# Second attention of a four-layer graph network: rows gathered per group of edges, block numbers loaded behind the next one-hot

## The chip, the cores and the metric

One NeuronCore of a Trainium2 chip runs the whole network as one program. The metric is the time of one execution on the device in microseconds (us), the median of some runs. Five engines work side by side, each with an instruction stream of its own and waiting for the others on semaphores: TensorE (PE, matrix products and transposes), VectorE (DVE), ScalarE (ACT), GpSimd (POOL, which here issues the gathers of rows) and SyncE (SP, plain DMAs).

## The reference

3125 nodes with 128 features, 50000 edges sorted by their target node. Four layers follow one another; the first two are attentions over edges:

```python
# first attention, H = 2 heads of 128
xl, xr = (h @ Wl + bl), (h @ Wr + br)
e = leaky_relu(xl[src] + xr[dst], 0.2)
alpha = segment_softmax(einsum('ehd,hd->eh', e, att), dst)
out = segment_sum(xl[src] * alpha[..., None], dst).mean(axis=1)
# second attention, one head
m = leaky_relu(xl[src] + xr[dst] + edge_weight @ We, 0.2)
alpha = segment_softmax(m @ att, dst)
out = segment_sum(xl[src] * alpha[:, None], dst)
```

Three GINE layers (message `relu(x[src] + e)`, sum by target, two dense layers, a batch norm) and an edge network with a node network end it. Each layer is followed by a residual sum and a layer norm.

## The kernel before

The edges are cut into 98 groups of 512. The nodes are cut into 25 blocks of 128. An item is a group together with one block of targets: a group whose targets cross from one block to the next is worked on twice, and so there are 98 + 24 = 122 items. `groups_blocks` holds for item i the group, its place in a ring of eight (`group & 7`), the block, and the block of item i - 2 (for the accumulation that lags two items). `group_end` holds for each group the number of items up to its last.

An attention (`gat_edges`, number 0 with two heads, number 1 with one) runs all 122 items in a pipeline that `walk` writes out: five items in full, then a loop with four items a turn, then the last. On each engine a step does `front` of item i, `tail` of item i - 2, `back` of item i - 1 and `mid` of item i. For one item and head:

- GpSimd gathers the source rows of 4 x 128 edges with four indirect DMAs (L760) into one of four buffers, after the products (L807) of the item four before have read it. An item that shares its group with the one before gathers the same rows again.
- TensorE transposes the rows (L772), ScalarE copies the transposes to `vs` (L820). TensorE adds the target side as three products with a one-hot matrix `hot_t` and, in the second attention, the edge weight (L780, L782).
- VectorE adds the two (L881, "the sum"), applies the leak (L885), makes the one-hot matrix of the next item (L863). TensorE multiplies by the attention vector (L790, "the scores").
- VectorE masks the scores and takes their maximum (L894, "the masked maximum"), and brings the running maximum up to date in three small steps (L901, L904, L906), whose addresses depend on the item's block number. ScalarE takes exponentials (L837, L840), TensorE transposes them (L799), ScalarE copies (L844), TensorE multiplies them with the gathered rows (L807), VectorE accumulates rows and sums into the place of the block (L917, L918). ScalarE makes the mask of the next item (L825).

VectorE needs the block numbers of items i and i - 2 as registers for these addresses. `read_blocks` (L865 to L873) loads both at once from `groups_blocks`; its instructions carry L871. It stands in `front` between the sum and the leak of the first head. L182 and L188 are lines of the helpers `wait` and `hold`, which issue waits and bring their values into registers.

In the GINE layers (L988) the rows are already gathered once per group into `ring`, the same memory seen as eight places of 4 x 128 rows of 128 features.

Of the kernel before, what the change touches and what calls it, by code (L numbers as in the profile page):

```python
# [23 lines left out]
ACT = mybir.ActivationFunctionType  # L24
AX = mybir.AxisListType.X

P = 128
NODES, EDGES, D = 3125, 50000, 128
EDGE_D, HID, HEADS, GINE_LAYERS = 32, 256, 2, 3
NODE_BLOCKS = -(-NODES // P)  # L30
# [3 lines left out]
SUBS = 4  # L34
# [48 lines left out]
def build(nc, t):  # L83

    with ExitStack() as ctx:
# [3 lines left out]
        def sem(name):  # L89
            return ctx.enter_context(nc.semaphore(name))  # L90
# [616 lines left out]
        rel_in = [sem(f"rel_in{s}") for s in range(2)]  # L707
        gathered = [sem(f"gathered{s}") for s in range(4)]


# [4 lines left out]
        def gat_edges(number, heads, dram, att, with_weight, target, sp_head=None, dve_head=None):  # L715
# [4 lines left out]
            name = f"gat{number}"  # L720
            w_in = [sem(f"{name}_w_in{s}") for s in range(2)] if with_weight else []
            cleared, hot_t_done, negs, g_ready, g_copied, v_ready, v_added, leaked, s_ready, s_masked, neg_max_new, max_step, max_done, p_ready, scl_ready, \
                pt_ready, pt_copied, o_ready, acc_done = gat_sems
# [10 lines left out]
            with nc.Block() as block:  # L734
# [20 lines left out]
                @block.gpsimd  # L755
                def _(pool):
                    for i in range(ITEMS):
                        wait(pool, o_ready, before_h + heads * (i - 3))
                        for j in range(SUBS):
                            pool.indirect_dma_start(  # L760
                                out=gath[:, i % 4, j, 0:width], out_offset=None, in_=dram,
                                in_offset=bass.IndirectOffsetOnAxis(ap=idx_all[:, i, j:j + 1], axis=0)).then_inc(gathered[i % 4], 16)

                @block.tensor
                def _(e):
                    def front(i, s, turn, s4, turn4):

                        e.wait_ge(gathered[s4], 16 * SUBS * (turn4 + 1))
                        for h in range(heads):
                            wait(e, pt_copied, before_h + heads * (i - 2) + h + 1)  # L770
                            for j in range(SUBS):
                                last = e.transpose(T[h][:, j * P:(j + 1) * P], gath[:, s4, j, h * D:(h + 1) * D], ident)  # L772
                            last.then_inc(g_ready, 1)
# [28 lines left out]
                    def tail(i, s, turn, s4, turn4):  # L802
                        wait(e, acc_done, before + i)
                        for h in range(heads):
                            e.wait_ge(pt_copied, before_h + heads * i + h + 1)
                            for j in range(SUBS):
                                last = e.matmul(O[h], pt[:, h, j, :], gath[:, s4, j, h * D:(h + 1) * D],  # L807
                                                start=(j == 0), stop=(j == SUBS - 1))
                            last.then_inc(o_ready, 1)
# [5 lines left out]
                def _(a):  # L815
                    def front(i, s, turn, s4, turn4):
                        for h in range(heads):
                            wait(a, leaked, before_h + heads * (i - 1) + h + 1)
                            a.wait_ge(g_ready, before_h + heads * i + h + 1)
                            a.activation(vs[:, h, :], T[h], ACT.Copy).then_inc(g_copied, 1)  # L820

                    def mask(i, s, turn):
# [4 lines left out]
                    def mid(i, s, turn, s4, turn4):  # L827

                        if not (isinstance(i, int) and i == ITEMS - 1):
                            mask(i + 1, 1 - s, turn + s)  # L830

                    def back(i, s, turn, s4, turn4):
# [13 lines left out]
                    target.scalar(a)  # L846
                    mask(0, 0, number * PAIRS)
                    walk(a, front, back, mid, layer=number)

                @block.vector  # L850
                def _(v):
# [23 lines left out]
                    def front(i, s, turn, s4, turn4):  # L875

                        for h in range(heads):
# [3 lines left out]
                            v.tensor_tensor(vs[:, h, :], V[h], vs[:, h, :], ALU.add).then_inc(v_added, 1)  # L881
                            if h == 0:
                                read_blocks(i)
                            v.wait_ge(v_added, before_h + heads * i + h + 1)
                            v.scalar_tensor_tensor(lk[:, h, :], vs[:, h, :], 0.2, vs[:, h, :], ALU.mult, ALU.max).then_inc(leaked, 1)  # L885
                        if not (isinstance(i, int) and i == ITEMS - 1):
                            make_hot_t(i + 1, 1 - s, turn + s)

                    def mid(i, s, turn, s4, turn4):
# [38 lines left out]
        gi_ea = [sem(f"gine_ea_in{s}") for s in range(2)]  # L928
        gi_gath = [sem(f"gine_gathered{s}") for s in range(RING)]
        gi_landed, gi_free = sem("gine_landed"), sem("gine_free")  # L930
# [7 lines left out]
        def gine_edges(layer):  # L938
# [8 lines left out]
            with nc.Block() as block:  # L947
                def landings(slot, round):

                    return 16 * SUBS * (layer * -(-(GROUPS - slot) // RING) + round + 1)  # L950

# [119 lines left out]
        def mlp_edges(target):  # L1071
# [4 lines left out]
            ea_before, rel_before = 16 * GINE_LAYERS * PAIRS, 16 * 2 * PAIRS  # L1076
            gathered_before = [16 * SUBS * 2 * -(-(ITEMS - m) // 4) for m in range(4)]
            cleared, hot_t_done, hot_done, counted, h1_ready, h1_added, turned, h1_done, h2_ready, h2_added, h2_done, o_ready, acc_step = (
# [819 lines left out]
```

## Time and profile before

| | us |
|---|---|
| median of 3 runs (lowest, highest) | 4297.36 (4291.48, 4302.65) |
| the profiled execution, its own time | 4295.06 |
| its span, first to last instruction | 4293.3 |
| busy in the span: PE, DVE, POOL, ACT | 3411.3, 2638.0, 2554.6, 1615.8 |
| first attention, sums from 106.2 on, last leak at | 911.5 |
| second attention, first leak, last leak at | 990.5, 1602.4 |

The span covers all layers one after another, so a share of busy time over the span is a mean over stages with different limits. The windows of a stage, the waits in it and the timeline of single items are read for what holds within the stage. An engine's name with a q at its end (DVEq, POOLq) is its sequencer: waits, register steps and loads, which aren't counted as busy.

### The profile page before, as it was taken

To read this page: it belongs to the slowest core of one execution; us is meant where nothing else is said; L and a number is where in the kernel's file an instruction comes from. 1 tells how busy PE (TensorE), PEld (TensorE's weight loads), DVE (VectorE), ACT (ScalarE), POOL (GpSimd) and SP (SyncE) were. 2 spreads that over 40 slices of the span, in tenths; PEclk is the share of its full clock that TensorE was granted. 3 is DMA by queue.
4 is the path that set the end of the run, shared out by engine and by line. 5 is a ranking of instruction groups with operands and counts; after the bars stand their busy time and mean duration, and the time that the engine had idled before them with its cause. 6 is when DMAs were issued, how large, how long until landed. Compare 5 with 4: busy or idle time off the path is not lost. (4 is left out here: it accounts for less than half of the span.)

```text
span 4293.3 us, 91716 instructions
## 1 busy us (share of the span) xinstructions
PE 3411.3 (79%) x20792; PEld 2646.5 (62%) x20793; DVE 2638.0 (61%) x6163; ACT 1615.8 (38%) x3137; POOL 2554.6 (60%) x2650
## 2 busy tenths in 40 slices
PE   6999999977788774676656566666666999999996
PEld 3777777754555543555545445455544888888894
DVE  5888888875666664343334333343345888888884
ACT  3666666644555553111121111211114333333334
POOL 4555555536777766777757777577772444444430
PEclk7999999988999995555566655555567999999998
DMA  3333333322322221222222222222222333333330
GB/s 118 89 98 100 100 99 99 101 69 63 80 80 81 80 70 57 68 68 68 67 62 68 67 67 68 60 69 69 67 68 73 112 107 107 111 107 107 111 90 15
DMA packets 293250, 349.78 MB, mean 81 GB/s; under 512 B 63536, under 2 KB 236755, under 8 KB 292915
## 3 DMA queue, kind: packets, MB, share of 16 engines
q0 software_dynamic: 98528, 229.12, 18.7%
q1 hardware_dynamic: 140481, 92.05, 7.8%
q10 hardware_dynamic: 54162, 27.77, 2.3%
q8 instruction: 24, 0.39, 0.0%
q14 instruction: 55, 0.45, 0.0%
HBM read 332.61 MB, written 16.07 MB: 81 GB/s over the span
## 5 line engine op out<-in xcount | busy, mean ns | idle before, releaser
L988 POOL DMA_INDIRECT gath<-source_rows_narrow,gine_idx x1176 | 1141.9, 971 | 426.7 <-issue 357.4
L1036 DVE TENSOR_TENSOR vs<-psum,gath 128x512 f32<-128x512 f32 x366 | 252.9, 691 | 802.3 <-SPq L973 673.7
L1142 POOL DMA_INDIRECT gath<-source_rows,idx_all x416 | 429.5, 1032 | 507.6 <-DVE vs L1263 351.9
L1002 PE MATMUL psum<-gine_lin,ea 32*128 32x128 f32 x2928 | 278.7, 468 | 543.2 <-DVE vs L1036 513.6
L760 POOL DMA_INDIRECT gath<-source_rows,idx_all x488 | 463.7, 950 | 378.1 <-PE psum L807 263.2
L760 POOL DMA_INDIRECT gath<-source_rows_narrow,idx_all x488 | 463.4, 950 | 207.1 <-issue 134.8
L1002 PEld LDWEIGHTS psum<-gine_lin,ea 32*128 32x128 f32 x2928 | 177.4, 286 | 642.0 <-DVE vs L1036 574.7
L790 PE MATMUL psum<-lk,att_b 128*128 128x512 f32 x732 | 376.4, 621 | 113.9 <-DVE lk L885 113.2
L807 PEld LDWEIGHTS psum<-gath,pt 128*128 128x128 f32 x2928 | 365.1, 192 | 36.8 <-DVE zsum L918 1.8
L1066 ACT ACTIVATE pm<-vs 128x512 f32<-128x512 f32 x186 | 117.1, 630 | 693.3 <-DVE vs L1036 686.6
L1167 PE MATMUL psum<-weight_all,pm 128*128 128x256 f32 x1664 | 377.2, 380 | 0.0
L1011 PE MATMUL psum<-hot,pm 128*128 128x128 f32 x1488 | 355.9, 414 | 19.9 <-ACT pm L1066 19.0
L807 PE MATMUL psum<-gath,pt 128*128 128x128 f32 x2928 | 366.4, 275 | 0.8 <-ACT pt L844 0.8
L1011 PE MATMUL psum<-lk,sm 128*128 128x128 f32 x1440 | 350.4, 420 | 4.4 <-ACT sm L1066 3.1
L885 DVE SCALAR_TENSOR_TENSOR lk<-vs 128x512 f32<-128x512 f32 x366 | 253.4, 692 | 160.1 <-DVE vs L881 150.9
L1011 PEld LDWEIGHTS psum<-hot,pm 128*128 128x128 f32 x1488 | 305.1, 304 | 63.1 <-DVE ACC L1045 46.8
L1066 ACT ACTIVATE sm<-vs 128x512 f32<-128x512 f32 x180 | 113.4, 630 | 607.9 <-DVE vs L1036 546.0
L1167 PEld LDWEIGHTS psum<-weight_all,pm 128*128 128x128 f32 x1664 | 308.7, 191 | 39.0
L1011 PEld LDWEIGHTS psum<-lk,sm 128*128 128x128 f32 x1440 | 301.4, 310 | 45.1 <-ACT sm L1066 20.8
L820 ACT ACTIVATE vs<-psum 128x512 f32<-128x512 f32 x366 | 205.4, 595 | 290.5 <-PE psum L772 290.5
L844 ACT ACTIVATE pt<-psum 128x512 f32<-128x512 f32 x366 | 205.5, 595 | 270.2 <-PE psum L799 261.0
L894 DVE CUSTOM_DVE_ANT_0 sm<-psum,neg 128x512 f32<-128x512 f32 x366 | 244.8, 686 | 94.2 <-PE psum L790 91.6
(241 smaller groups left out, 6143.6 us busy)
## 6 DMA issues: line engine op xcount, KB each, us to landing
rel<-rel_rows SPq DMA_DIRECT2D x244, 128.0 KB
ea<-in_edge_attr_tiles SPq DMA_DIRECT2D x416, 64.0 KB
ea<-in_edge_attr ACTq DMA_DIRECT2D x366, 64.0 KB
gath<-source_rows_narrow,gine_idx POOLq DMA_INDIRECT x1176
gath<-source_rows,idx_all POOLq DMA_INDIRECT x904
rel<-quad_rel_rows SPq DMA_DIRECT2D x104, 128.0 KB
gath<-source_rows_narrow,idx_all POOLq DMA_INDIRECT x488
source_rows<-ACC SPq DMA_DIRECT2D x12, 512.0 KB, 2.9
```

The costliest lines, as they stand in the source:

```text
L760: pool.indirect_dma_start(out=gath[:, i % 4, j, 0:width], out_offset=None, in_=dram, in_offset=bass.IndirectOffsetOnAxis(ap=idx_all[:, i, ...
L790: e.matmul(S[h], att_b[:, att[h], :], lk[:, h, :], start=True, stop=True).then_inc(s_ready, 1)
L807: last = e.matmul(O[h], pt[:, h, j, :], gath[:, s4, j, h * D:(h + 1) * D], start=(j == 0), stop=(j == SUBS - 1))
L885: v.scalar_tensor_tensor(lk[:, h, :], vs[:, h, :], 0.2, vs[:, h, :], ALU.mult, ALU.max).then_inc(leaked, 1)
L894: v.tensor_tensor_reduce(out=sm[:, h, :], in0=S[h], in1=neg[:, s, :], scale=1.0, scalar=-4 * MASK, op0=ALU.subtract, op1=ALU.max, accum_ou ...
L988: pool.indirect_dma_start(out=ring[:, g % RING, j, :], out_offset=None, in_=table1, in_offset=bass.IndirectOffsetOnAxis(ap=gine_idx[:, g, ...
L1002: last = e.matmul(E[:, j, :], ea[rows, s, :], gine_lin[rows, layer, :], start=True, stop=True)
L1011: last = e.matmul(O[s4], pms[s4][:, j * P:(j + 1) * P], hots[s4][:, j, :], start=(j == 0), stop=(j == SUBS - 1))
L1036: v.tensor_tensor(vs[:, s, :].rearrange("p (j d) -> p j d", j=SUBS), E, ring[:, bass.ds(slot, 1), :, :].rearrange("p a j d -> p (a j) d"), ...
L1066: a.activation(pms[s4], vs[:, s, :], ACT.Relu).then_inc(gi["msg"], 1)
L1142: pool.indirect_dma_start(out=gath[:, q % 4, j, :], out_offset=None, in_=table, in_offset=bass.IndirectOffsetOnAxis(ap=quad_idx[:, q, j:j ...
L1167: last = e.matmul(H2[:, j, :], h1[:, h, j * P:(j + 1) * P], w2[h], start=(h == 0), stop=(h == 1))
```

## The change

In the second attention GpSimd gathers each group once, into the ring of eight, in 4 indirect DMAs for each of 98 groups. Ahead of a group's gathers (from the ninth group on) it loads the group's last item and waits until that item's rows are taken; behind them it waits for the group before to land and says so (`rows_landed`). ScalarE copies an item's rows from the ring to one of four buffers (`rows`, in the unused half of `ACC`), one item ahead, behind the copy of the transposes. It loads the item's group and ring place ahead of that copy. TensorE reads the rows from there. In both attentions `read_blocks` moves from between the first head's sum and leak to behind the next item's one-hot. The waits of later layers are renumbered.

```diff
--- before.py
+++ after.py
@@ -706,6 +706,8 @@
 
         rel_in = [sem(f"rel_in{s}") for s in range(2)]
         gathered = [sem(f"gathered{s}") for s in range(4)]
+        gi_gath = [sem(f"group_gathered{s}") for s in range(RING)]
+        rows_landed, rows_taken, slot_free = (sem(f"gat1_{k}") for k in ("rows_landed", "rows_taken", "slot_free"))
 
 
         gat_sems = [sem(f"gat_{k}") for k in (
@@ -719,6 +721,8 @@
             acc = ACC[:, 0:NODE_BLOCKS * width].rearrange("p (b h d) -> p b h d", h=heads, d=D)
             name = f"gat{number}"
             w_in = [sem(f"{name}_w_in{s}") for s in range(2)] if with_weight else []
+            by_group = heads == 1
+            rows = ACC[:, NODE_BLOCKS * D:NODE_BLOCKS * D + 4 * GROUP_EDGES].rearrange("p (s j d) -> p s j d", s=4, j=SUBS) if by_group else gath
             cleared, hot_t_done, negs, g_ready, g_copied, v_ready, v_added, leaked, s_ready, s_masked, neg_max_new, max_step, max_done, p_ready, scl_ready, \
                 pt_ready, pt_copied, o_ready, acc_done = gat_sems
             before = number * ITEMS
@@ -754,6 +758,25 @@
 
                 @block.gpsimd
                 def _(pool):
+                    def report(g):
+                        pool.wait_ge(gi_gath[g % RING], 16 * SUBS * (g // RING + 1))
+                        pool.nop().then_inc(rows_landed, 1)
+
+                    if by_group:
+                        pool.wait_ge(gine_idx_in, 16)
+                        for g in range(GROUPS):
+                            if g >= RING:
+                                end = pool.value_load(group_end[0:1, g - RING:g - RING + 1], min_val=1, max_val=ITEMS)
+                                pool.wait_ge(rows_taken, end)
+                                pool.nop().then_inc(slot_free, 1)
+                            for j in range(SUBS):
+                                pool.indirect_dma_start(
+                                    out=ring[:, g % RING, j, :], out_offset=None, in_=dram,
+                                    in_offset=bass.IndirectOffsetOnAxis(ap=gine_idx[:, g, j:j + 1], axis=0)).then_inc(gi_gath[g % RING], 16)
+                            if g >= 1:
+                                report(g - 1)
+                        report(GROUPS - 1)
+                        return
                     for i in range(ITEMS):
                         wait(pool, o_ready, before_h + heads * (i - 3))
                         for j in range(SUBS):
@@ -765,11 +788,14 @@
                 def _(e):
                     def front(i, s, turn, s4, turn4):
 
-                        e.wait_ge(gathered[s4], 16 * SUBS * (turn4 + 1))
+                        if by_group:
+                            e.wait_ge(rows_taken, i + 1)
+                        else:
+                            e.wait_ge(gathered[s4], 16 * SUBS * (turn4 + 1))
                         for h in range(heads):
                             wait(e, pt_copied, before_h + heads * (i - 2) + h + 1)
                             for j in range(SUBS):
-                                last = e.transpose(T[h][:, j * P:(j + 1) * P], gath[:, s4, j, h * D:(h + 1) * D], ident)
+                                last = e.transpose(T[h][:, j * P:(j + 1) * P], rows[:, s4, j, h * D:(h + 1) * D], ident)
                             last.then_inc(g_ready, 1)
 
                         b = block_of(e, i)
@@ -804,7 +830,7 @@
                         for h in range(heads):
                             e.wait_ge(pt_copied, before_h + heads * i + h + 1)
                             for j in range(SUBS):
-                                last = e.matmul(O[h], pt[:, h, j, :], gath[:, s4, j, h * D:(h + 1) * D],
+                                last = e.matmul(O[h], pt[:, h, j, :], rows[:, s4, j, h * D:(h + 1) * D],
                                                 start=(j == 0), stop=(j == SUBS - 1))
                             last.then_inc(o_ready, 1)
 
@@ -814,10 +840,15 @@
                 @block.scalar
                 def _(a):
                     def front(i, s, turn, s4, turn4):
+                        taken = by_group and not (isinstance(i, int) and i == ITEMS - 1)
+                        if taken:
+                            place_of_rows = load_place(i + 1)
                         for h in range(heads):
                             wait(a, leaked, before_h + heads * (i - 1) + h + 1)
                             a.wait_ge(g_ready, before_h + heads * i + h + 1)
                             a.activation(vs[:, h, :], T[h], ACT.Copy).then_inc(g_copied, 1)
+                        if taken:
+                            take(i + 1, (s4 + 1) % 4, *place_of_rows)
 
                     def mask(i, s, turn):
                         a.wait_ge(rel_in[s], 16 * (turn + 1))
@@ -828,6 +859,19 @@
 
                         if not (isinstance(i, int) and i == ITEMS - 1):
                             mask(i + 1, 1 - s, turn + s)
+
+                    def load_place(i):
+                        _, (g, slot) = nc.values_load_multi_w_load_instructions(
+                            groups_blocks[0:1, bass.ds(i, 1), 0:2], engines=(mybir.EngineType.Activation,),
+                            min_val=0, max_val=GROUPS - 1)
+                        return g, nc.s_assert_within(slot, 0, RING - 1)
+
+                    def take(i, s4, g, slot):
+                        a.wait_ge(rows_landed, g + 1)
+                        if not isinstance(i, int) or i >= 4:
+                            a.wait_ge(o_ready, before_h + i - 3)
+                        a.activation(rows[:, s4, :, :], ring[:, bass.ds(slot, 1), :, :].rearrange("p a j d -> p (a j) d"),
+                                     ACT.Copy).then_inc(rows_taken, 1)
 
                     def back(i, s, turn, s4, turn4):
 
@@ -845,6 +889,8 @@
 
                     target.scalar(a)
                     mask(0, 0, number * PAIRS)
+                    if by_group:
+                        take(0, 0, *load_place(0))
                     walk(a, front, back, mid, layer=number)
 
                 @block.vector
@@ -879,12 +925,11 @@
                             v.wait_ge(v_ready, before_h + heads * i + h + 1)
                             v.wait_ge(g_copied, before_h + heads * i + h + 1)
                             v.tensor_tensor(vs[:, h, :], V[h], vs[:, h, :], ALU.add).then_inc(v_added, 1)
-                            if h == 0:
-                                read_blocks(i)
                             v.wait_ge(v_added, before_h + heads * i + h + 1)
                             v.scalar_tensor_tensor(lk[:, h, :], vs[:, h, :], 0.2, vs[:, h, :], ALU.mult, ALU.max).then_inc(leaked, 1)
                         if not (isinstance(i, int) and i == ITEMS - 1):
                             make_hot_t(i + 1, 1 - s, turn + s)
+                        read_blocks(i)
 
                     def mid(i, s, turn, s4, turn4):
                         b = blocks["item"]
@@ -926,7 +971,6 @@
         gi = {k: sem(f"gine_{k}") for k in (
             "hot_done", "e_ready", "added", "msg", "o_ready", "acc_done", "cleared")}
         gi_ea = [sem(f"gine_ea_in{s}") for s in range(2)]
-        gi_gath = [sem(f"gine_gathered{s}") for s in range(RING)]
         gi_landed, gi_free = sem("gine_landed"), sem("gine_free")
 
         def group_of(e, i):
@@ -947,7 +991,7 @@
             with nc.Block() as block:
                 def landings(slot, round):
 
-                    return 16 * SUBS * (layer * -(-(GROUPS - slot) // RING) + round + 1)
+                    return 16 * SUBS * ((layer + 1) * -(-(GROUPS - slot) // RING) + round + 1)
 
                 def by_group(e, body):
 
@@ -1074,7 +1118,7 @@
             acc = ACC[:, :].rearrange("p (h b n) -> p b h n", h=2, n=P)
             ea_in = gi_ea
             ea_before, rel_before = 16 * GINE_LAYERS * PAIRS, 16 * 2 * PAIRS
-            gathered_before = [16 * SUBS * 2 * -(-(ITEMS - m) // 4) for m in range(4)]
+            gathered_before = [16 * SUBS * -(-(ITEMS - m) // 4) for m in range(4)]
             cleared, hot_t_done, hot_done, counted, h1_ready, h1_added, turned, h1_done, h2_ready, h2_added, h2_done, o_ready, acc_step = (
                 sem(f"mlp_{k}") for k in ("cleared", "hot_t_done", "hot_done", "counted", "h1_ready", "h1_added", "turned", "h1_done", "h2_ready", "h2_added",
                                           "h2_done", "o_ready", "acc_step"))
```

## Rows read from the trace of the kernel before

**Rows 1.** Windows view, both attentions: us; busy PE, PEld, DVE, ACT, POOL; clock, DMA share, GB/s.
```profile
97.00:902.00 805.00, 794.47 (x5012) 585.71 (x5013) 660.53 (x1917) 514.27 (x1198) 447.30 (x472) 0.99 0.35 97
970.00:1607.00 637.00, 504.82 (x2714) 317.24 (x2713) 399.96 (x1232) 336.15 (x742) 454.78 (x479) 0.98 0.29 76
```

**Rows 2.** Waits view, second attention: waiter, releaser, total us, times, longest.
```profile
DVE lk L885 <- DVE vs L881: 77.2, 119, 1.0
```

**Rows 3.** Timeline of VectorE, four items of the first attention: start, us.
```profile
502.38 0.69 DVE L881 TENSOR_TENSOR vs<-psum,vs 128x512 f32<-128x512 f32 x1
...
512.08 0.69 DVE L885 SCALAR_TENSOR_TENSOR lk<-vs 128x512 f32<-128x512 f32 x1
...
515.89 0.69 DVE L881 TENSOR_TENSOR vs<-psum,vs 128x512 f32<-128x512 f32 x1
517.21 0.69 DVE L885 SCALAR_TENSOR_TENSOR lk<-vs 128x512 f32<-128x512 f32 x1 [0.62 <-DVE vs L881]
517.81 0.68 DVE L881 TENSOR_TENSOR vs<-psum,vs 128x512 f32<-128x512 f32 x1
518.53 0.69 DVE L885 SCALAR_TENSOR_TENSOR lk<-vs 128x512 f32<-128x512 f32 x1
...
520.18 0.68 DVE L894 CUSTOM_DVE_ANT_0 sm<-psum,neg 128x512 f32<-128x512 f32 x1
...
522.32 0.69 DVE L881 TENSOR_TENSOR vs<-psum,vs 128x512 f32<-128x512 f32 x1
...
528.72 0.69 DVE L881 TENSOR_TENSOR vs<-psum,vs 128x512 f32<-128x512 f32 x1
```

**Rows 4.** Line L871, VectorE's sequencer, 515.8 to 517.2: ns min/median/max, first, last start.
```profile
L871 DVEq FUSED_REGOPS  x3: 81/197/209, 515.9 to 516.9; - x3
...
L871 DVEq TENSOR_LOAD <-groups_blocks x1: 530/530/530, 516.0 to 516.0; - x1
```

**Rows 5.** Lines L188 and L182 on VectorE's sequencer, five narrow windows.
```profile
L188 DVEq FUSED_REGOPS  x1: 154/154/154, 513.2 to 513.2; - x1
...
L188 DVEq FUSED_REGOPS  x1: 154/154/154, 519.4 to 519.4; - x1
...
L182 DVEq EVENT_SEMAPHORE  x1: 50/50/50, 519.7 to 519.7; - x1
...
L188 DVEq FUSED_REGOPS  x1: 154/154/154, 1286.1 to 1286.1; - x1
...
L188 DVEq FUSED_REGOPS  x1: 154/154/154, 1301.6 to 1301.6; - x1
```

**Rows 6.** Timeline, second attention: VectorE over four items, then all engines, 1286 to 1289.
```profile
1284.21 0.69 DVE L881 TENSOR_TENSOR vs<-psum,vs 128x512 f32<-128x512 f32 x1
...
1287.57 0.69 DVE L894 CUSTOM_DVE_ANT_0 sm<-psum,neg 128x512 f32<-128x512 f32 x1 [0.70 <-PE psum L790]
...
1289.07 0.69 DVE L881 TENSOR_TENSOR vs<-psum,vs 128x512 f32<-128x512 f32 x1
...
1300.69 0.69 DVE L885 SCALAR_TENSOR_TENSOR lk<-vs 128x512 f32<-128x512 f32 x1 [0.62 <-DVE vs L881]
...
1304.33 0.69 DVE L881 TENSOR_TENSOR vs<-psum,vs 128x512 f32<-128x512 f32 x1
...
1286.27 1.13 PE L790 MATMUL psum<-lk,att_b 128*128 128x512 f32 x2 [0.84 <-DVE lk L885]
...
1286.47 0.94 POOL L760 DMA_INDIRECT gath<-source_rows_narrow,idx_all  x1 [0.30 <-issue]
...
1287.87 0.60 ACT L820 ACTIVATE vs<-psum 128x512 f32<-128x512 f32 x1 [1.20 <-PE psum L772]
...
1288.61 0.72 ACT L837 ACTIVATE pm<-sm,small 128x512 f32<-128x512 f32 x1
```

**Rows 7.** Lines L947 and L988: end of the first edge layer on GpSimd.
```profile
L947 POOLq DRAIN  x1: 19265/19265/19265, 2141.0 to 2141.0; - x1
...
L988 POOL DMA_INDIRECT gath<-source_rows_narrow,gine_idx x392: 940/945/2119, 1656.9 to 2155.0; - x196
```

## Prediction

> **What bounds the kernel now.** I read the windows of the two attentions first, then the waits of VectorE in them, then the timeline of single items, then the sequencer's own instructions. In the first attention TensorE is busy for 794 of 805 us, in the second for 505 of 637, with the clock fully granted in both [rows 1]. So at first sight TensorE bounds the first attention and something else the second. The waits and the timelines show one pause that both share: the leak (L885) waits for the sum before it (L881) once an item, for some 77 us in total in the second, 0.62 us a time in both [rows 2, 3, 6]. That isn't the sum's latency, because the second head has the same pair without a pause (517.81 to 518.53 is the sum's own 0.68 us) [rows 3]. It is the load of two block numbers: its instructions begin at 515.9, right behind the sum, and go on into the second half of the pause [rows 3, 4].
>
> Of one item of the first attention the reader should see VectorE's order: sum, leak, sum, leak, next one-hot, two pairs of accumulations (L917, L918), then the two masked maxima (L894), then the three small steps, and the next sum. The item begun at 515.89 has its first masked maximum at 520.18 (4.29 later), and the next item begins at 522.32 (2.14 after that): 6.43. VectorE's only pause of size in it is the 0.62 [rows 3]. Four items (one turn of the loop) take 528.72 - 502.38 = 26.34, 6.585 each, so three items go at VectorE's 6.4 and the one with the loop's branch takes 7.06. TensorE's own work is at most 794.47 / 122 = 6.51 an item [rows 1]. The first attention is bound by both engines at once, and VectorE has nothing to give away.
>
> In the second attention four items take 1304.33 - 1284.21 = 20.12, or 5.03 each [rows 6]. The ring of one item is: sum, load, leak, scores on TensorE (L790, 1286.27), the next item's transposes (L772) and products (L782) behind them, the next sum at 1289.07. A gather costs GpSimd 0.94 and 0.30 of issue, 1.245, and four of them 4.98 [rows 6]: GpSimd is a second bound, 0.05 behind the first. Neither half of the change would bring much by itself there.
>
> **GpSimd, part by part.** 488 gathers become 392: 98 groups x 4.98 = 488 us, from 959 us on, 4.0 for each of the 122 items. Each group adds one load of a number, two waits and two signals. The load that the trace prices, VectorE's, takes 1.26 for two numbers (from 515.9 until the leak is issued at 517.2) [rows 3, 4]. From below it is free: the closing drain of the first edge layer starts on GpSimd's sequencer at 2141.0, while the last gather starts at 2155.0, so the sequencer runs eleven gathers ahead of the engine [rows 7], and the wait for the group before ends while the engine still has gathers of this group. From above the whole 1.26 is exposed: 98 x 6.24 = 612, 5.01 an item, and the gain of this attention is gone. I take free, for the sequencer's lead is shown. 5.0 to 4.0 takes GpSimd off the path.
>
> **ScalarE.** It gains one copy of 128x512 in each item of the second attention, and a load of two numbers. The nearest row for the copy is the transposed rows' copy, 0.60 [rows 6]. It goes behind that copy (L820) and ahead of the exponential (L837), which now starts 0.74 after L820. Counted from the item's first sum in the new ring: scores at 1.46, L820 1.60 after them (1286.27 to 1287.87) at 3.06, the new copy to 4.3, the exponential and its sum 0.82 (estimate from its 0.72) to 5.15, its four transposes, 0.65 with their start, to 5.9. The next scores stand behind them on TensorE and are due at 4.78 + 1.46 = 6.24. So 0.3 are left, and the copy is covered. The loads lie under the mask of 0.71 and in the idle 1.20 ahead of L820 [rows 6]. The copy's wait for the group has a ring of eight groups ahead of it. ScalarE's busy time goes from 336 by 122 x 0.6 = 73 to 409 of 637 [rows 1]: not a bound. Price 0; if the copy came onto the ring in full, +0.6 an item, which is the upper end. TensorE waits for this copy in place of the gather, one item ahead. Its first copy adds under 1 us at the start, hidden by VectorE's clearing of the accumulator.
>
> **VectorE, the decisive part.** The load leaves the place between sum and leak and goes behind the issue of the next one-hot. Between these places VectorE's sequencer waits for the last sum, so its lead is gone when the load begins; behind the load stand the waits and address steps of the accumulations and of the masked maximum. The sequencer does one after the other. Its time there: the last leak starts at 518.53, the address step L188 ahead of the masked maximum at 519.4, 0.87 later, and an item before 512.08 and 513.2, 1.12. I take the middle, 0.99. In the second attention it is 0.91 (1300.69 to 1301.6) and 0.58 (1286.1, with the leak 0.74 ahead of its scores at 1286.27), the middle 0.74 [rows 3, 5, 6]. L188 takes 0.154; the wait behind it starts at 519.7, 0.3 after L188; and the masked maximum starts about 0.13 later (estimate, from 1287.57 and its wait) [rows 5]. So 0.43 from L188 to the masked maximum.
>
> First attention, from the item's first sum: leak at 0.73, second sum at 0.73 + 0.60, last leak at 2.05 (from 517.21, 517.81, 518.53), then 0.99 + 1.26 + 0.43: masked maximum at 4.73 where it is at 4.29. The 0.6 is gained ahead of the last leak, but the engine then runs dry under the load (one-hot done at about 3.0, first accumulation at 3.8). +0.44 an item; in the loop's branch item some 0.12 of waiting for the second head's scores drops out, 0.03 an item. TensorE, ACT and GpSimd follow. 121 x 0.41 = **+50 us**.
>
> Second attention: leak at 0.73, masked maximum at 0.73 + 0.74 + 1.26 + 0.43 = 3.16 where it is 3.36 (1284.21 to 1287.57); the next sum 1.50 after it (1287.57 to 1289.07), and 0.12 for the branch (0.47 in one of four): 4.78 in place of 5.03. TensorE's ring would allow less: 0.73 + 0.72 + 2.80 = 4.25, 4.39 with the branch. 108 items x 0.25 = 27; the first twelve pay a further 5 for gathers that come late, which the ring of eight takes away. **-32 us.**
>
> Sum +18 on the profiled execution's 4295.06 (span 4293.3 and 1.8 around it), which is 2.3 under the median of three: 4315 us on the median's basis.
>
> A load of two numbers takes 0.530 on VectorE's sequencer, without the address steps around it [rows 4]. The Trainium skill ("DMA: Bandwidth & Descriptors", section "Latency and other measured facts") puts the floor of a tensor_load at about 600 ns; the row is under it. By the page the load behind the one-hot would be 0.07 longer in each of 229 items, 16 us more than by the row; the row is of the same instruction, and decides.
>
> **Rivals.** About 0.3% (13 us) is what a measurement of this kernel can tell from no change.
> A, forecast: the load is serial on the sequencer in both attentions, +50 - 32. With +-0.07 an item on some 240 items 4298 to 4332. Chance 0.50, 0.15 of it within 0.3%, whose upper end is 4310.
> B: it is serial, but my sequencer distances are 0.1 to 0.2 too long, for address steps may be cheaper behind a load. Each 0.1 is worth 24 us over both attentions, +18 - 36 in the middle: 4279, 4267 to 4300. For it: the distances differ by 0.25 to 0.33 between items of one loop. Chance 0.24, 0.16 of it within 0.3%.
> C, the other side: the load lies wholly under the leak and one-hot (0.60 + 0.35 of engine time against 1.26) and the idle 0.70 ahead of the masked maximum. Then the first attention goes at TensorE's pace, 26.34 to some 26.18 per four items, -5 us, and the second at TensorE's 4.39: 108 x 0.64 + 10 = -79. 4213. It decides where the load leaves the masked maximum where it was. For it: the second attention has that idle time. Against: the first has none, and there its 0.31 beyond the engine time and 0.9 of steps behind it can't hide. Chance 0.18, with parts of it up to 4262.
> D: GpSimd's load or ScalarE's copy is exposed, the second attention gains nothing: 4297 + 50 = 4347, past the upper end of the range. Chance 0.08.
>
> **Numbers.** Predicted 4315. The range, 4260 to 4338, leaves out C's core and D. Slower by over 0.3%: A 0.35 and D 0.08, 0.43. Within: A 0.15 and B 0.16, 0.31. Faster: B 0.08 and C 0.18, 0.26.
>
> **What would show it.** The leak's pause gone in both (0.62 to nothing); in its place a pause of VectorE between the one-hot and the first accumulation, some 0.8 in the first attention. Four items of the first attention in 28.0, of the second in 19.1. TensorE's busy share of the first falls from 0.99. GpSimd waits for the ring in the second. If the first attention keeps 26.3, the step on the sequencer is wrong; if the second keeps 20, look at the exponential and the new copy.

## The result, and the profile after

The changed kernel takes 4306.28 us (median of 15 runs, 4300.59 to 4309.84), the kernel before, beside it on the same chip, 4296.24 (15 runs, 4291.41 to 4302.65): a ratio of 1.0021, 95% interval 1.0014 to 1.0028. That is 10 us slower: clear of the scatter of the runs, but within the 0.3% that the prediction counts as no change. Predicted were +18 us and "slower by over 0.3%" as the likeliest. The time lies in the stated range; the change is not the one that was held likeliest.

The windows of the changed kernel, cut at the same places of the work as those of [rows 1] (columns as there):
```profile
97.00:943.00 846.00, 819.67 (x4961) 579.74 (x5021) 677.09 (x1919) 528.18 (x1201) 467.91 (x472) 0.99 0.34 92
1010.00:1617.00 607.00, 515.79 (x2683) 320.24 (x2714) 414.09 (x1231) 396.05 (x865) 372.53 (x384) 0.98 0.28 70
```
Beside [rows 1], the first window has grown by 41 us and the second has shrunk by 30. From the first sum to the last, it is 802.7 to 842.9 us (+40.3) in the first attention and 611.5 to 581.9 (-29.6) in the second. In the second GpSimd's busy time falls from 455 to 373 us, for 98 groups in place of 122 items, and ScalarE's rises from 336 to 396, for the copies out of the ring. Two effects of opposite sign stand behind a total that looks like nothing. In the first window TensorE's busy time grows from 794 to 820 us for the same products, so busy time isn't a fixed amount of work. The 794 of 805 in [rows 1] doesn't by itself show TensorE's own pace; the run with the load taken apart, below, does.

VectorE's timeline, one item of the first attention (lines have moved: the sum is L927, the leak L929, the one-hot L909, the accumulations L962 and L963, the masked maximum L939, the load of the block numbers L917):
```profile
522.94 0.69 DVE L927 TENSOR_TENSOR vs<-psum,vs 128x512 f32<-128x512 f32 x1
523.66 0.69 DVE L929 SCALAR_TENSOR_TENSOR lk<-vs 128x512 f32<-128x512 f32 x1
524.27 0.68 DVE L927 TENSOR_TENSOR vs<-psum,vs 128x512 f32<-128x512 f32 x1
524.99 0.69 DVE L929 SCALAR_TENSOR_TENSOR lk<-vs 128x512 f32<-128x512 f32 x1
525.60 0.35 DVE L909 TENSOR_SCALAR hot_t<-rel,consts 128x512 bf16<-128x512 bf16 x1
526.81 0.35 DVE L962 SCALAR_TENSOR_TENSOR ACC<-ACC,factors,psum 128x128 f32 x1 [0.86 <-issue]
...
527.66 0.69 DVE L939 CUSTOM_DVE_ANT_0 sm<-psum,neg 128x512 f32<-128x512 f32 x1
...
530.31 0.69 DVE L927 TENSOR_TENSOR vs<-psum,vs 128x512 f32<-128x512 f32 x1 [0.55 <-issue]
...
550.84 0.69 DVE L927 TENSOR_TENSOR vs<-psum,vs 128x512 f32<-128x512 f32 x1
```
The 0.62 between sum and leak of [rows 3] is gone: the first leak starts 0.72 after its sum. Behind the one-hot stands a new pause of 0.86, from 525.95 to 526.81, released by "issue": VectorE's own sequencer isn't ready. The load and its steps take the sequencer from 525.24 to 526.47:
```profile
L917 DVEq FUSED_REGOPS  x3: 75/197/209, 525.2 to 526.2; - x3
...
L917 DVEq TENSOR_LOAD <-groups_blocks x1: 527/527/527, 525.4 to 525.4; - x1
```
The load itself (0.53 from 525.35) still runs under the last leak and the one-hot. What falls into the pause are its address steps (525.91 to 526.47) and, behind them on the same sequencer, the waits and the address step of the first accumulation.

Four items, 522.94 to 550.84, take 27.90, from 26.34 before. In the second attention one item reads:
```profile
1319.57 0.69 DVE L927 TENSOR_TENSOR vs<-psum,vs 128x512 f32<-128x512 f32 x1
1320.30 0.69 DVE L929 SCALAR_TENSOR_TENSOR lk<-vs 128x512 f32<-128x512 f32 x1
1320.91 0.35 DVE L909 TENSOR_SCALAR hot_t<-rel,consts 128x512 bf16<-128x512 bf16 x1
1322.12 0.35 DVE L962 SCALAR_TENSOR_TENSOR ACC<-ACC,factors,psum 128x128 f32 x1 [0.87 <-issue]
...
1322.71 0.69 DVE L939 CUSTOM_DVE_ANT_0 sm<-psum,neg 128x512 f32<-128x512 f32 x1
...
1324.67 0.69 DVE L927 TENSOR_TENSOR vs<-psum,vs 128x512 f32<-128x512 f32 x1 [0.50 <-PE psum L808]
...
1338.74 0.69 DVE L927 TENSOR_TENSOR vs<-psum,vs 128x512 f32<-128x512 f32 x1
```
The masked maximum comes 3.14 after the sum (3.36 in [rows 6]), and four items, 1319.57 to 1338.74, take 19.17, from 20.12. The waits of the second attention agree:
```profile
DVE ACC L962 <- issue: 103.6, 120, 1.2
...
POOL gath L773 <- ACT ACC L873: 74.2, 40, 4.1
```
The 77 us in front of the leak [rows 2] are gone and 104 us in front of the first accumulation have come. That the item is shorter all the same comes from the masked maximum: in the kernel before VectorE waits for its scores as well, 0.70 in [rows 6], 86.7 us in the whole window of the second attention; in the changed kernel these waits are down to 5.2.
```profile
DVE sm L894 <- PE psum L790: 86.7, 121, 2.0
```
The scores now start 0.6 earlier, with the leak, and are ready when the sequencer is. The leak's pause and this wait shrink by more than the new pause costs. GpSimd now waits for a free place in the ring (L873 is ScalarE's copy out of it): it is off the path.

### The profile page after: what moved, and what is told of

Its sections match the earlier page's. It is cut to its first block and busy times, and to the rows that moved or that the text cites. A ratio compares the mean times of both kernels' runs of the same rounds, so it can differ in the third digit from the quotient of the medians.

```text
span 4298.8 us, 93469 instructions
## 1 busy us (share of the span) xinstructions
PE 3466.9 (81%) x20700; PEld 2662.1 (62%) x20793; DVE 2668.6 (62%) x6163; ACT 1687.9 (39%) x3259; POOL 2491.2 (58%) x2554
## 5 line engine op out<-in xcount | busy, mean ns | idle before, releaser
L1032 POOL DMA_INDIRECT gath<-source_rows_narrow,gine_idx x1176 | 1140.7, 970 | 426.3 <-issue 357.5
L1186 POOL DMA_INDIRECT gath<-source_rows,idx_all x416 | 429.5, 1033 | 507.1 <-DVE vs L1307 352.0
L783 POOL DMA_INDIRECT gath<-source_rows,idx_all x488 | 484.3, 992 | 399.2 <-PE psum L833 284.6
L773 POOL DMA_INDIRECT gath<-source_rows_narrow,gine_idx x392 | 380.4, 971 | 217.3 <-issue 99.3
L816 PE MATMUL psum<-lk,att_b 128*128 128x512 f32 x732 | 400.0, 634 | 60.2 <-DVE lk L929 59.3
L1055 PE MATMUL psum<-hot,pm 128*128 128x128 f32 x1488 | 367.0, 424 | 18.0 <-ACT pm L1110 17.6
L1055 PEld LDWEIGHTS psum<-hot,pm 128*128 128x128 f32 x1488 | 314.9, 313 | 61.3 <-DVE ACC L1089 43.4
L881 ACT ACTIVATE pm<-sm,small 128x512 f32<-128x512 f32 x366 | 262.0, 716 | 122.5 <-DVE small L946 119.0
L927 DVE TENSOR_TENSOR vs<-psum,vs 128x512 f32<-128x512 f32 x366 | 252.3, 689 | 41.3 <-PE psum L808 18.8
L808 PE MATMUL psum<-hot_t,XR 128*128 128x512 bf16 x1006 | 259.5, 382 | 15.9 <-DVE hot_t L909 5.8
L929 DVE SCALAR_TENSOR_TENSOR lk<-vs 128x512 f32<-128x512 f32 x366 | 254.2, 695 | 12.5
```

The source lines that it names most:

```text
L773: pool.indirect_dma_start(out=ring[:, g % RING, j, :], out_offset=None, in_=dram, in_offset=bass.IndirectOffsetOnAxis(ap=gine_idx[:, g, j: ...
L783: pool.indirect_dma_start(out=gath[:, i % 4, j, 0:width], out_offset=None, in_=dram, in_offset=bass.IndirectOffsetOnAxis(ap=idx_all[:, i, ...
L808: last = e.matmul(V[h], XR[:, bass.ds(b, 1), k, h * D:(h + 1) * D].rearrange("p a d -> p (a d)"), hot_t[:, s, :], start=(k == 0 and not wi ...
L816: e.matmul(S[h], att_b[:, att[h], :], lk[:, h, :], start=True, stop=True).then_inc(s_ready, 1)
L881: a.activation(pm[:, h, :], sm[:, h, :], ACT.Exp, bias=NEGM[:, h:h + 1], accum_out=ZI[s][:, h:h + 1]).then_inc(p_ready, 1)
L1032: pool.indirect_dma_start(out=ring[:, g % RING, j, :], out_offset=None, in_=table1, in_offset=bass.IndirectOffsetOnAxis(ap=gine_idx[:, g, ...
```

## The experiments

Each kernel was timed beside the kernel before on one chip. "After" is the changed kernel. "Four items" is the time from the sum of one item to that of the fourth behind it, as read above, in the steady part of the loop (the middle value over the loop's turns). Where a text below speaks of a whole attention, it is the time from its first sum to its last in the profiled execution; before, 802.7 and 611.5 us.

**Each half alone.** After, with the load back between sum and leak:
```diff
                             v.tensor_tensor(vs[:, h, :], V[h], vs[:, h, :], ALU.add).then_inc(v_added, 1)
+                            if h == 0:
+                                read_blocks(i)
...
                             make_hot_t(i + 1, 1 - s, turn + s)
-                        read_blocks(i)
```


> The gathers per group and ScalarE's copy, with the load of the two block numbers back at its old place between sum and leak in both attentions. Theory (the load is serial work of VectorE's sequencer, and the gathers alone free a GpSimd that was only 0.05 us an item behind): the first attention is back at 26.34 us for four items, the second stays near the 20.12 of the kernel before, 20.0 to 20.1, with some 5 us less at its start; 4290 against 4296. Rival (the gain of the second attention is GpSimd's, not the load's): the second attention at 19.2 as in the changed kernel, 4266.

Measured: 4297.46 us, ratio 1.0001 (0.9992 to 1.0010); four items 26.35 and 20.19. The gather per group alone brings nothing: with GpSimd's 4.98 an item gone, VectorE's 5.03 remains. I had allowed it 5 us in the first items of the second attention, and it doesn't give those either.

The kernel before, with the load behind the one-hot and nothing else:
```diff
                             v.tensor_tensor(vs[:, h, :], V[h], vs[:, h, :], ALU.add).then_inc(v_added, 1)
-                            if h == 0:
-                                read_blocks(i)
...
                             make_hot_t(i + 1, 1 - s, turn + s)
+                        read_blocks(i)
```


> The kernel before with only the load moved behind the next one-hot in both attentions, gathers per item as before. Theory: first attention at 27.9 for four items (+41), second held by GpSimd's four gathers, 4 x 1.245 = 4.98 an item or 19.9 to 20.0 for four (-3 in all): 4334. Rival (VectorE's move alone makes the second attention's gain): 19.2 there, -30, 4307.

Measured: 4341.47 us, ratio 1.0106 (1.0090 to 1.0121); four items 27.90 and 20.29. The first attention is that of after (843.3 us, +40.6), so its loss is the load's. The second is not 3 us shorter, as expected, but 3.5 longer: the gain doesn't come, for TensorE's transposes (L772) now wait for the gathers, as the waits between 1030 and 1650 us say (6.2 us of this wait in the kernel before):
```profile
PEld psum L772 <- DMA gath<-source_rows_narrow,idx_all: 80.5, 89, 2.1
```

**The load moved in the second attention only**, gathers per group:
```diff
+                            if h == 0 and not by_group:
+                                read_blocks(i)
...
-                        read_blocks(i)
+                        if by_group:
+                            read_blocks(i)
```


> The changed kernel with the load at its old place in the first attention and behind the one-hot in the second. Theory: the first attention at 26.34 for four items, the second at 19.17: 41 us under the changed kernel, 30 under the one before, 4266. Rival (part of the first attention's loss comes from elsewhere, a shift of the code or the later waits): the first attention stays above 26.8 for four items.

Measured: 4264.59 us, ratio 0.9921 (0.9908 to 0.9935); four items 26.35 and 19.17. With the first attention as before (802.9 us), the rest of the change is worth -32 us by the medians, of which the second attention has 28.7 in the profiled execution. The difference to after, 4306.28 - 4264.59 = 42, is the price of the move in the first (40.0 in the profiled executions).

**The load taken apart**, gathers per group. The item's number alone behind the first head's sum; the number two items back behind the second head's sum in the first attention, behind the one-hot in the second:
```diff
-                        if isinstance(i, int) and i < 2:
-                            blocks["item"] = block_of(v, i)
-                        else:
-                            _, (blocks["item"], blocks["tail"]) = nc.values_load_multi_w_load_instructions(...)
+                        blocks["item"] = block_of(v, i)
+
+                    def read_tail(i):
+                        if not isinstance(i, int) or i >= 2:
+                            blocks["tail"] = v.value_load(groups_blocks[0:1, bass.ds(i, 1), 3], ...)
...
                             v.tensor_tensor(vs[:, h, :], V[h], vs[:, h, :], ALU.add).then_inc(v_added, 1)
+                            if h == 0:
+                                read_blocks(i)
+                            else:
+                                read_tail(i)
...
-                        read_blocks(i)
+                        if heads == 1:
+                            read_tail(i)
```


> The changed kernel with the one load of two numbers split into two loads of one number: the item's block number behind the first head's sum; that of the item two back behind the second head's sum (first attention) or behind the next one-hot (second). A load of one number takes 0.30 us, with its steps 0.64 (lines L936 of the traces), which fits under a sum of 0.69. Theory (only what sticks out of the running instruction costs): no pause before the leak and none behind the one-hot of the first attention, which goes to TensorE's 26.2 for four items (-5 against the kernel before); the second goes to the ring through TensorE and ScalarE, 4.40 to 4.45 an item or 17.6 to 17.8 for four, -72 to -78; together 4213 to 4219. Rival (two loads cost the sequencer two issues and it is the number of its steps that counts): both attentions within 1% of the changed kernel's best stage each, 4260 to 4270.

Measured: 4228.97 us, ratio 0.9840 (0.9827 to 0.9854); four items 26.18 and 18.05. It is faster than both kernels. VectorE in the first attention:
```profile
497.98 0.69 DVE L926 TENSOR_TENSOR vs<-psum,vs 128x512 f32<-128x512 f32 x1
498.76 0.69 DVE L932 SCALAR_TENSOR_TENSOR lk<-vs 128x512 f32<-128x512 f32 x1
499.37 0.68 DVE L926 TENSOR_TENSOR vs<-psum,vs 128x512 f32<-128x512 f32 x1
500.09 0.69 DVE L932 SCALAR_TENSOR_TENSOR lk<-vs 128x512 f32<-128x512 f32 x1
500.70 0.35 DVE L909 TENSOR_SCALAR hot_t<-rel,consts 128x512 bf16<-128x512 bf16 x1
500.96 0.34 DVE L966 SCALAR_TENSOR_TENSOR ACC<-ACC,factors,psum 128x128 f32 x1
...
502.16 0.69 DVE L943 CUSTOM_DVE_ANT_0 sm<-psum,neg 128x512 f32<-128x512 f32 x1 [0.34 <-PE psum L816]
```
A load of one number fits under one sum: the leak comes 0.78 after it, 0.06 later than with no load. The second one (on the sequencer from 498.98 to 499.65) runs while the engine has the first leak and the second sum to do, both issued ahead of it. Neither leaves the engine a pause of its own. What VectorE waits for now is TensorE, 45 us for scores (L816) and 15 for products between 110 and 890 us, while TensorE waits 8 us for leaks: 26.18 is TensorE's pace. The loop of the first attention gains only 4 us by it, the whole attention 9 (793.8 us). The 13 us by which the forecast's middle missed lie in the second attention: 4.51 an item in place of 4.4.

**The load taken apart, gathers per item.** The same edit on the kernel before.

> The kernel before, gathers per item and no copy of the ring, with the load taken apart: the item's number behind the first head's sum, the number two items back behind the second head's sum in the first attention and behind the one-hot in the second. Theory that the second attention is held by two things at once, VectorE's chain and GpSimd's four gathers of 4.98 us an item: the first attention goes as with the split load, four items in 26.2, and the second stays at GpSimd's pace, four items in 20.0 to 20.3; about 4290 us. Rival, GpSimd is no bound and VectorE's chain is all: four items of the second in 18.05 as with the gathers per group, about 4229 us.

Measured: 4295.16 us, ratio 1.0007 (0.9997 to 1.0017); four items 26.18 and 20.29. The same edit that is worth 4297.46 - 4228.97 = 68 us on top of the gathers per group is worth nothing without them. In the first attention it gives 8 us either way (802.7 to 794.7 here, 802.3 to 793.8 there); the difference is all in the second, 611.5 to 617.6 here, 613.0 to 548.6 there. GpSimd is shown as the bound of the second, by the waits and the busy time of the 480 us from 1100 to 1580:
```profile
POOL gath L760 <- issue: 108.8, 357, 0.3
...
PEld psum L772 <- DMA gath<-source_rows_narrow,idx_all: 61.4, 70, 1.3
```
```profile
1100.00:1580.00 480.00, 395.49 (x2085) 233.78 (x2085) 312.93 (x943) 248.23 (x568) 364.00 (x379) 1.00 0.32 80
```
364.00 busy and 108.8 in gaps of 0.3 make 473 of 480 us: GpSimd goes from gather to gather. Why it then takes 5.07 an item, and not the 4.98 of four gathers, is not shown.

**ScalarE's room.** After, with ScalarE's load of group and ring place behind its first copy, not ahead of it:
```diff
-                        if taken:
-                            place_of_rows = load_place(i + 1)
...
-                            take(i + 1, (s4 + 1) % 4, *place_of_rows)
+                            take(i + 1, (s4 + 1) % 4, *load_place(i + 1))
```


> The kernel after, with ScalarE's load of the group's and the slot's number moved from ahead of the first copy (of the transposed rows) to behind it, right ahead of the copy out of the ring. Theory that ScalarE has some 0.3 us an item to spare in the second attention and that a load of two numbers with its steps is about 1.1 to 1.25 us of sequencer time, of which the copy covers 0.6: the exponential comes 0.5 later, 0.1 to 0.3 an item is exposed, four items of the second in 19.6 to 20.3, 4320 to 4336 us. Rival, ScalarE is not near the path and VectorE's 4.79 an item stays: 19.2, 4306 us. The first attention keeps 27.9.

Measured: 4332.33 us, ratio 1.0096 (1.0079 to 1.0113); four items 27.89 and 20.03. One item of it, ScalarE and then TensorE, where VectorE's sum is at 1343.39:
```profile
1343.29 0.63 ACT L871 ACTIVATE ACC<-gath 128x512 f32 x1 [0.90 <-issue]
1343.83 0.71 ACT L879 ACTIVATE pm<-sm,small 128x512 f32<-128x512 f32 x1
...
1344.75 0.65 PE L825 MATMUL psum<-consts,pm 128*128 128x128 f32 x4 [0.52 <-ACT pm L879]
1345.24 1.02 PE L816 MATMUL psum<-lk,att_b 128*128 128x512 f32 x2
...
1347.27 0.37 PE L806 MATMUL psum<-wrow,we_parts 9*128 9x512 bf16 x1 [0.46 <-issue]
```
and the same item of after, where the sum is at 1329.54:
```profile
1329.17 0.72 ACT L881 ACTIVATE pm<-sm,small 128x512 f32<-128x512 f32 x1 [0.31 <-DVE small L946]
...
1330.11 0.65 PE L825 MATMUL psum<-consts,pm 128*128 128x128 f32 x4 [0.44 <-ACT pm L881]
1331.02 1.12 PE L816 MATMUL psum<-lk,att_b 128*128 128x512 f32 x2 [0.25 <-DVE lk L929]
```
Counted from the sum, the exponential (L879, L881) comes 0.44 behind it in place of 0.37 ahead, 0.81 later. TensorE's scores (L816) then go at 1.85 in place of 1.48, held by the exponential's transposes ahead of them on the same engine. (20.03 - 19.17) / 4 = 0.22 an item comes through. So after has a few tenths to spare on this path, as the prediction had it, and where the load of the place stands decides whether that is enough.

**The load twice.** After, with `read_blocks(i)` doubled behind the one-hot:
```diff
                         read_blocks(i)
+                        read_blocks(i)
```


> The kernel after, with VectorE's load of the two block numbers done twice behind the one-hot, in both attentions. Theory that the load is serial on VectorE's sequencer with nothing over it once the one-hot has been issued: 1.2 us more an item in both, four items of the first in 32.8, of the second in 24.1, about 4305 + 121 x 1.23 + 121 x 1.23 = 4600 us. Rival, that the load lies largely under the leak and the one-hot and only the wait for them costs: 0.6 or less more an item, under 4450 us.

Measured: 4581.44 us, ratio 1.0675 (1.0654 to 1.0696); four items 32.43 and 23.77. That is (32.43 - 27.90) / 4 = 1.13 and (23.77 - 19.17) / 4 = 1.15 an item: the second load costs its whole sequencer time. VectorE in the first attention:
```profile
590.74 0.35 DVE L909 TENSOR_SCALAR hot_t<-rel,consts 128x512 bf16<-128x512 bf16 x1
593.05 0.35 DVE L963 SCALAR_TENSOR_TENSOR ACC<-ACC,factors,psum 128x128 f32 x1 [1.96 <-issue]
```
The pause of 0.86 has become 1.96. The second load is serial in both attentions, and the rival of a load that is largely hidden (0.6 or less an item) falls. The forecast of 1.23 an item was a little too high.

## Where the prediction was right, and the term that it mis-sized

**What bounds the kernel.** Right. The pause ahead of the leak was the load: it is gone where the load is moved or taken apart. Both engines bound the first attention: taking VectorE's pause away altogether (the load taken apart) gives 26.18, TensorE's pace, where the kernel before takes 26.34, so TensorE stood only 0.04 an item behind. That GpSimd stands right behind VectorE's ring in the second attention is shown by the runs with one half each. The gathers alone give +1 us. The load moved alone gives +45, of which 41 are the first attention's. The load taken apart alone gives +4, not told apart from no change. Only both halves together bring the gain of the second attention.

**GpSimd and ScalarE at nothing.** Right. GpSimd has time to wait for the ring. All 90 of its loads (L769) start 1.1 to 2.9 us before the last gather already issued does, so they lie where gathers are still queued. The copy out of the ring holds no one up in the loop. Rival D is out, though the run with the late place load shows how it would have come about: ScalarE 0.8 later costs 0.22 an item.

**VectorE in the second attention, -32.** Right in its mechanism, and near in size. Predicted were the leak at 0.73, the masked maximum at 3.16 and four items in 19.1; measured 0.73, 3.14 in the item shown (3.15 on the mean of a turn) and 19.17. The 108 items of the middle give -27.5, where 27 was predicted, but the whole attention -29.6: of the "further 5" for late gathers in the first items only 2 are left. The second item takes 6.83 in place of 4.33. In it the exponential stands behind ScalarE's new copy out of the ring (0.62) and comes 1.2 behind the item's sum, where it came with it, and the scores take 1.91 in place of 1.12, at a granted clock of 0.75 on the mean of the item in place of 1.00. So the copy, priced at 0, isn't free there. In the run with the gathers per group alone that item takes 7.07, and the whole attention 613.0: the 5 us don't come at all.

**VectorE in the first attention, +50.** This is the step that failed: the mechanism is right, but "121 x 0.41 = +50 us" is too large, and the attention lost 40.3. The distances held: in the four items of a turn the masked maximum stands at 4.73, 4.88, 4.57 and 4.69, on the mean 4.72, where 4.73 was predicted, and the first accumulation at 3.9, where 3.8 was. The 108 items in the middle rose by 0.389 each in place of 0.41, 42.0 us in place of 44. Most of the miss is in the factor 121, which gave the loop's price to all items: the 13 items at the two ends did not pay 5 us but gained 1.7. Four of the first five keep their time to 0.03. The other places are two.

The item begun at 111.9 fell from 8.58 to 6.88. Its scores are four matmuls, before (L790) and after (L816), and the windows give TensorE's busy time and its granted clock, the kernel before first:
```profile
115.29 3.51 PE L790 MATMUL psum<-lk,att_b 128*128 128x512 f32 x4
...
116.00 1.88 PE L816 MATMUL psum<-lk,att_b 128*128 128x512 f32 x4
```
```profile
115.40:118.80 3.40, 3.40 (x6) 1.23 (x5) 0.70 (x2) 1.21 (x2) 0.00 (x0) 0.50 0.10 28
...
115.40:118.80 3.40, 3.35 (x18) 2.17 (x18) 1.63 (x5) 2.28 (x6) 0.00 (x0) 1.00 0.03 9
```
In the kernel before the granted clock of TensorE is 0.50, its lower level (1.2 GHz), for these 3.4 us. The scores take 3.51 in place of 1.88, and VectorE waits longer for them ahead of both masked maxima. In after the clock stays at the upper level. The same holds in all nine traces: with the load in its old place (three of them) the clock falls there and the item takes 8.57 or 8.58; with the load moved or taken apart (six) it doesn't fall and the item takes 6.88. TensorE does nearly the same ahead of it in both, with a pause of 1.6 us in front of the exponential's transposes; why the clock falls in the one and not in the other is not shown.

The other place is the last turn of the loop. In its third item VectorE's load itself takes 4124 ns in the kernel before and 1720 in after, where the same instruction takes 530 in the turns before. The time from the sum of the last item but two to that of the last is 17.7 us in the kernel before, 17.3 and 17.7 in the other two with the load in its old place, and 15.2 to 15.3 in the three with the load moved whole and done once. These last two steps became 2.5 us shorter in after, where the loop's price would have made them 0.8 longer: 3.3 of the 9.7 us of the miss. That goes with the load's place in all of these kernels, with one profiled execution of each. What makes the load slow is not shown.

**The total.** 40.3 - 29.6 is +10.7, and the medians say +10.0. The two profiled executions differ by only 5.5 (spans 4293.3 and 4298.8), for the stretches outside the two attentions differ by -5.2. Between the nine profiled executions these stretches lie 5.5 below to 5.2 above those of the kernel before, so that is not read as the change's.

**Rivals.** C, a load wholly hidden, is refuted by the pause and by the doubled load. B, distances 0.1 to 0.2 too long, is refuted, for the masked maximum came where it was put, and 4306 lies above its range. The time lies in A's own range, in the part within 0.3% that was given 0.15. The forecast was the difference of two nearly equal terms, +50 and -32: an error of a fifth in the first carried it over the 0.3% line. That the total lies inside the range is no proof of the terms; the distances and the four items are.

## What to carry to other kernels

Loading numbers into an engine's registers costs that engine's sequencer time: in this kernel 1.13 to 1.15 us for two numbers with their steps (the load done twice), 1.24 from the first step to the last (before). Only work that was issued to the engine ahead of it, and still runs, covers it. Put the load behind an instruction at least as long as the load with its steps, and if none is long enough, cut it in two behind two of them: here, with the gathers per group, that is -1.6%, where moving it whole is +0.2%. Where two engines stand within a per cent of each other, test both edits together, for each alone can bring nothing. And price a pipeline's first and last items apart from its loop: here 13 of 122 items held 7 of the 10 us of the miss in the first attention.

## What the runs showed of the hardware that was not expected

A load of one number takes about 290 ns: a median of 294 on VectorE and of 291 on TensorE (both L736) in the run with the load taken apart, 284 to 298 on GpSimd in after. Two numbers in one load take 527 to 530 on VectorE and 492 on ScalarE. The Trainium skill ("DMA: Bandwidth & Descriptors", section "Latency and other measured facts") puts the floor of a tensor_load at about 600 ns; all these rows lie under it, and the measurement decides. What counts is the load with the address steps around it: the doubled load measures it as 1.13 to 1.15 us for two numbers.

In the last turn of the first attention's loop one load on VectorE takes far longer than the same instruction in the turns before. In all nine traces VectorE's slowest load stands there: 1.6 to 4.1 us for two numbers, 1.2 for one. In the second attention none on VectorE takes over 0.6 us. What makes it slow, no run here tells.

Whether TensorE's granted clock fell to its lower level (0.50) for 3.4 us at the start of the first attention went with where VectorE's load stood, in nine traces of nine. Where it fell, the item took 1.7 us more.
